# Spectral layer of a four-layer network: six block products for each full Toeplitz product, shifted differences subtracted by GpSimd

## What is computed

```python
U_plus  = causal_conv(phi[:, k], u)                  # u: 2304 tokens, phi: taps of filter k, 16 filters
U_minus = causal_conv(phi[:, k], u * sgn) * sgn      # sgn = +1, -1, +1, ...
out = sum_k s_k * (U_plus @ M_plus[k] + U_minus @ M_minus[k]) + sum_i shift(u, i) @ M_u[i]
# four such sums, on the first T, T/2, T/4 and T/8 tokens, with matrices of their own, are weighted and added
```

## Time and profile before

| what | value |
|---|---|
| three runs, median (lowest to highest) | 8442.53 us (8434.91 to 8447.69) |
| profiled execution: time, span | 8448.98 us, 8447.1 us |
| mean granted TensorE clock | 0.954 of full |
| busy share of the span: TensorE, VectorE, ScalarE, GpSimd | 91%, 63%, 45%, 43% |
| spectral layer, setup to last store | about 6097 to 8447 us |

### The profile page before, as it was taken

One profiled execution on the slowest core, in us unless ns is written; L12 is line 12 of the kernel. 1 busy time (PEld: TensorE's weight loads), 2 busy tenths in 40 slices (PEclk: granted clock), 3 DMA queues, 4 the chain that ended last, 5 costly groups with the idle time before them and its releaser, 6 DMA issues. The chain is left out here.

```text
span 8447.1 us, 141745 instructions
## 1 busy us (share of the span) xinstructions
PE 7665.0 (91%) x51342; PEld 5961.6 (71%) x51342; DVE 5345.4 (63%) x8084; ACT 3817.7 (45%) x8029; POOL 3663.7 (43%) x2420
## 2 busy tenths in 40 slices
PE   8999899997999979999467788699799999999999
PEld 6888678885888858887356677356666666666666
DVE  7999799996999969999445555455532222222222
ACT  5887578873888748876112222244421111111111
POOL 5888468882888828886355554110000000000000
PEclk9999999998999989999689899899999999999999
DMA  2333123331333313332565554000022222222222
GB/s 64 90 91 89 59 75 90 91 88 45 91 90 90 89 44 91 91 90 73 160 181 159 157 156 135 6 3 0 7 89 86 87 91 87 80 94 92 80 86 77
DMA packets 459084, 727.20 MB, mean 86 GB/s; under 512 B 51687, under 2 KB 364040, under 8 KB 456497
## 3 DMA queue, kind: packets, MB, share of 16 engines
q1 hardware_dynamic: 406705, 550.52, 21.1%
q0 software_dynamic: 51840, 169.91, 7.0%
HBM read 686.77 MB, written 33.46 MB: 85 GB/s over the span
## 5 line engine op out<-in xcount | busy, mean ns | idle before, releaser
L591 POOL TENSOR_TENSOR l_arena<-l_arena 128x768 f32<-128x768 f32 x1536 | 2778.7, 1824 | 472.0 <-DVE l_arena L541 411.2
L541 DVE TENSOR_TENSOR_SCAN l_arena<-l_arena,psum 128x384 f32<-128x384 f32 x3072 | 2866.4, 983 | 78.2 <-PE psum L382 42.8
L475 ACT ACTIVATE l_arena<-l_arena,l_A 128x384 f32<-128x384 f32 x3072 | 1665.3, 604 | 81.4 <-DVE l_arena L541 81.3
L384 PE MATMUL psum<-l_arena 128*128 128x128 f32 x11520 | 1581.2, 285 | 28.7 <-DVE l_arena L541 26.2
L384 PEld LDWEIGHTS psum<-l_arena 128*128 128x128 f32 x11520 | 1407.5, 192 | 184.9 <-issue 114.4
L2344 DVE TENSOR_TENSOR st_Uc<-psum,st_both 128x384 f32<-128x384 f32 x512 | 285.5, 558 | 1701.0 <-PE psum L2265 1701.0
L395 PE MATMUL psum<-l_ident,l_arena 128*128 128x128 f32 x9216 | 1260.2, 273 | 53.0 <-ACT l_yT L481 45.5
L395 PEld LDWEIGHTS psum<-l_ident,l_arena 128*128 128x128 f32 x9216 | 1053.7, 141 | 64.3 <-POOL l_arena L591 41.5
L2265 PE MATMUL psum<-st_F,st_xt 128*128 128x384 f16 (+2 forms) x6912 | 1002.1, 290 | 0.0
L2265 PEld LDWEIGHTS psum<-st_F,st_xt 128*128 128x128 f16 x6912 | 649.5, 97 | 385.3 <-issue 62.3
L1148 POOL DMA_INDIRECT l_G<-neighbours,l_idx x648 | 618.6, 955 | 665.4 <-PE psum L1196 325.0
(11 more groups left out here) (397 smaller groups left out, 7668.8 us busy)
## 6 DMA issues: line engine op xcount, KB each, us to landing
l_arena<-c_rows SPq DMA_DIRECT2D x1536, 192.0 KB, 3.0
st_FS<-filter_sums SPq DMA_DIRECT2D x128, 641.0 KB, 7.6
st_F<-filter_parts SPq DMA_DIRECT2D x128, 576.5 KB, 6.4
neighbours<-l_xt SPq DMA_DIRECT2D x256, 72.0 KB
st_mab<-in_st_mp SPq DMA_DIRECT2D x68, 256.0 KB, 7.6
st_mab<-in_st_mm SPq DMA_DIRECT2D x68, 256.0 KB, 7.9
l_G<-neighbours,l_idx POOLq DMA_INDIRECT x648
l_gnx<-in_x SPq DMA_DIRECT2D x4, 1152.0 KB, 5.9
```

The lines of the kernel that those rows point to most:

```text
L384: mm = pe.matmul(ps[:, o:o + P], dtuT[:, g % 2, t, h * P:(h + 1) * P], diagB[:, rank[s] % 3, t, :], start=True, stop=True)
L475: act.activation(decay[:, s % NDC, h, :], dtv[:, g % 2, h, :], ACT.Exp, scale=A[:, g // NRC, h, n:n + 1]).then_inc(s_exp, 1)
L541: dve.tensor_tensor_scan(hbuf[:, n, h, flip], decay[:, s % NDC, h, flip], ps[:, BANK * (2 * (s % 2) + h):BANK * (2 * (s % 2) + h) + RC][:, ...
L591: pool.tensor_tensor(hC[:, s % NHC], hbuf[:, s % NS], Cs[:, s % NCS, :].unsqueeze(1).broadcast_to([P, 2, RC]), ALU.mult).then_inc(s_hc, 1)
```

## The change

Each full product of 3 x 3 blocks is made of six block products. With block taps t(d) and token blocks x0, x1, x2, each row i of the result is t(i-0) x0 + t(i-1) x1 + t(i-2) x2. `own` takes one token block for each row, with the sum of three neighbouring block taps; `pairs` takes three differences of token blocks, each with one block of taps, and each of these three enters two rows, once added and once subtracted. So nine matmuls of 384 columns become 9 + 9 of 128. The results of `own` and of `pairs` lie in banks 5 and 6. The one of the two uses of `pairs` is added in place; the other is shifted by a block, and this *rotated* subtraction is GpSimd's: two `tensor_tensor`, 256 and 128 columns, on `Uc[:, 1]` and again on `Uc[:, 2]`.

The results of mixing now take banks 0 to 4 (the last third in three pieces of 128). The next unit's `shared` and `first` stand ahead of this unit's last mixing. The setup stores five sums of taps (rows of 512) instead of two; `F` shrinks from 1153 to 641 columns, `FS` grows from 2 x 641 to 5 x 385 (for each part, parity and buffer). The token differences (six sets of three blocks) are formed by GpSimd at each batch's start; ordering, transposes and cutting go 384 columns at a time, and ScalarE copies the tokens.

```diff
-FW = HL + 1
+FW = RC + 2 * P + 1
-SW = SR - P + 1
+SW = RC + 1
+SETS, SETW = 5, RC + P
...
             @block.vector
+                st.mark(dve.tensor_tensor(threes[:, 0], tap[:, 0:SETW], tap[:, P:P + SETW], ALU.add))
+                st.link(dve.tensor_tensor(threes[:, 1:3], sums[:, :, 0:SETW], sums[:, :, P:P + SETW], ALU.add))
+                st.mark(dve.tensor_tensor(threes[:, 0], threes[:, 0], tap[:, 2 * P:2 * P + SETW], ALU.add))
+                st.link(dve.tensor_tensor(threes[:, 1:3], threes[:, 1:3], sums[:, :, 2 * P:2 * P + SETW], ALU.add))
+                for at, n, of in ((0, 2, sums[:, :, P:P + SETW]), (2, 3, threes)):
+                    dve.tensor_copy(sets_h[:, at:at + n], of).then_inc(s_th, 1)
...
+                for at, n, of in ((0, 2, sums[:, :, P:P + SETW]), (2, 3, threes)):
+                    dve.tensor_tensor(sets_l[:, at:at + n], of, sets_h[:, at:at + n], ALU.subtract).then_inc(s_th, 1)
...
+                @block.gpsimd
+                def _(pool):
                     for q in range(2):
+                        pool.wait_ge(s_xc, b * 2 * LB + 3 + q)
+                        pool.tensor_tensor(xd[:, q, :], xr[:, q, 0:RC], xr[:, q, RC:2 * RC], ALU.subtract).then_inc(s_xd, 1)
+                    for q in range(2):
+                        src = xr[:, q, 0:2 * RC].rearrange("p (g j s) -> p g j s", g=2, j=LB)
+                        for e, (i, j) in enumerate(((1, 2), (0, 1), (2, 0))):
+                            pool.tensor_tensor(xe[q][:, 0:2, e], src[:, :, i], src[:, :, j], ALU.subtract).then_inc(s_xd, 1)
+                        pool.wait_ge(s_xd, b * 10 + 5 + 4 * q)
+                        pool.tensor_tensor(xe[q][:, 2], xe[q][:, 0], xe[q][:, 1], ALU.subtract).then_inc(s_xd, 1)
...
+                    def own(u, at, three, x0, start):
+
+                        r, z, q, shift = shape(u)
+                        for i in range(LB):
+                            for m, (xpart, fpart) in enumerate(PARTS):
+                                mm = pe.matmul(ps[:, at + i * P:at + (i + 1) * P], xt[:, xpart, x0 + LB - 1 - i, :],
+                                               FS[:, r, fpart, z, three, shift + i * P:shift + (i + 1) * P],
+                                               start=(start and i + m == 0), stop=(i == LB - 1 and m == 2), skip_group_check=True)
+                        return mm
+
+                    def pairs(u, tap, group, start):
+
+                        r, z, q, shift = shape(u)
+                        for e, d in enumerate((0, 2, 1)):
+                            for m, (xpart, fpart) in enumerate(PARTS):
+                                mm = pe.matmul(ps[:, PAIR + e * P:PAIR + (e + 1) * P], xt[:, xpart, PAIR0 + (3 * q + group) * 3 + e, :],
+                                               tap[:, r, fpart, z, shift + d * P:shift + (d + 1) * P],
+                                               start=(start and e + m == 0), stop=(e == 2 and m == 2), skip_group_check=True)
+                        return mm
...
+                        for u in range(2 * NU):
+                            r, q = u // NU, u % 2
+                            done, turned_on = (unit + u) * 4 + 8, (unit + u) * 4 + 4
+                            copied = (unit + u) * 4
+                            pe.wait_ge(s_ea, copied + 2)
+                            own(u, OWN, 3, q * HB + LB, False)
+                            pairs(u, FS[:, :, :, :, 0], 1, False).then_inc(s_cv, 1)
+                            if u % NU == 0:
+                                pe.wait_ge(s_wm[r], use(i, r) + 1)
+                            pe.wait_ge(s_ea, copied + 3)
+                            mix(u, 0)
+                            triangle(u, q * HB + 2 * LB)
+                            own(u, LOW, 4, q * HB, False).then_inc(s_cv, 1)
+                            pe.wait_ge(s_ea, copied + 4)
+                            pairs(u, FS[:, :, :, :, 1], 0, True).then_inc(s_cv, 1)
+                            pe.wait_ge(s_po, turned_on + 2)
+                            mix(u, 1)
+                            v = (u + 1) % (2 * NU)
+                            if not (last and v == 0):
+                                if v % NU == 0:
+                                    pe.wait_ge(s_fl[v // NU], (b * (KF // 2) + i + (1 if v else 2)) * 64)
+                                shared(v)
+                                pe.wait_ge(s_ed, done + 3)
+                                shared_pairs(v)
+                                first(v)
+                            pe.wait_ge(s_po, turned_on + 4)
+                            mm = mix(u, 2)
...
                 @block.vector
+                            dve.wait_ge(s_cv, (unit + u) * 5 + 3)
+                            dve.wait_ge(s_ea, (unit + u) * 4 + 4)
+                            dve.tensor_tensor(second, ps[:, OWN:OWN + RC], pair_1[:], ALU.add).then_inc(s_ed, 1)
+                            if step < 5:
+                                mix_step(i * 2 + r + 1, i + r, 1 - r, step, base + (i * 2 + r + 1) * 8)
+                            dve.wait_ge(s_cv, (unit + u) * 5 + 4)
+                            dve.tensor_tensor(third, ps[:, LOW:LOW + RC], own_s[:, u % 2, :], ALU.subtract).then_inc(s_ed, 1)
+                            dve.wait_ge(s_cv, (unit + u) * 5 + 5)
+                            dve.wait_ge(s_po, (unit + u) * 4 + 4)
+                            dve.tensor_tensor(pair_2[:], ps[:, PAIR:PAIR + RC], pair_s[:, u % 2, :], ALU.subtract).then_inc(s_ed, 1)
+                            dve.wait_ge(s_ed, at + 3)
+                            dve.tensor_tensor(third, third, pair_2[:], ALU.add).then_inc(s_ed, 1)
+                            if step + 1 < 5:
+                                mix_step(i * 2 + r + 1, i + r, 1 - r, step + 1, base + (i * 2 + r + 1) * 8)
...
+                @block.gpsimd
+                def _(pool):
+                    with pool.Fori(0, KF // 2) as i:
+                        unit = (b * KF + i * 2) * NU
+                        for u in range(2 * NU):
+                            for c, step, pair in ((1, 1, pair_1), (2, 4, pair_2)):
+                                pool.wait_ge(s_ed, (unit + u) * 4 + 8 + step)
+                                pool.tensor_tensor(Uc[:, c, P:], Uc[:, c, P:], pair[:, 0:2 * P], ALU.subtract).then_inc(s_po, 1)
+                                pool.tensor_tensor(Uc[:, c, 0:P], Uc[:, c, 0:P], pair[:, 2 * P:], ALU.subtract).then_inc(s_po, 1)
...
                 @block.scalar
+                            act.activation(own_s[:, u % 2, :], ps[:, OWN:OWN + RC], ACT.Copy).then_inc(s_ea, 1)
+                            act.activation(pair_s[:, u % 2, :], ps[:, PAIR:PAIR + RC], ACT.Copy).then_inc(s_ea, 1)
+                            act.wait_ge(s_cv, (unit + u) * 5 + 2)
+                            act.activation(Uc[:, 0, :], ps[:, LOW:LOW + RC], ACT.Copy).then_inc(s_ea, 1)
+                            act.wait_ge(s_cv, (unit + u) * 5 + 3)
+                            act.wait_ge(s_po, (unit + u) * 4 + 2)
+                            act.activation(pair_1[:], ps[:, PAIR:PAIR + RC], ACT.Copy).then_inc(s_ea, 1)
```

More of the change, by code:

```diff
@@ L2155, in pieces, with rows_of, place, totals @@
             return out
+        def rows_of(c):
+            return [(c * RC, (c + 1) * RC)] if c < 2 else [(2 * RC + i * P, 2 * RC + (i + 1) * P) for i in range(3)]
+        def place(p, x):
+            if x < 2 * RC:
+                return BANK * (2 * p + x // RC) + x % RC
+            n = (x - 2 * RC) // P
+            return (BANK * (2 * p + n) + RC if n < 2 else BANK * 4 + P * p) + x % P
+        def totals(p, c):
+            return [(m, lo, hi, place(p, lo)) for r0, r1 in rows_of(c) for m, lo, hi in pieces(r0, r1)]
         with nc.Fori(0, NB) as b:
@@ L2198, in layer3_spectral @@
             with nc.Block() as block:
-                NU, KINDS = 4, ("shared", "first", "second", "third")
-                NG = NU * len(KINDS)
+                NU = 4
+                OWN, PAIR, LOW = (BANK * i for i in (5, 6, 7))
                 USES = (KF // 2 + 1, KF // 2)
@@ new lines, in _, with shape, triangle @@
+                    PARTS = ((0, 0), (0, 1), (1, 0))
+                    def shape(u):
+                        r, z, q = u // NU, u // 2 % 2, u % 2
+                        return r, z, q, (0 if (z and q) else 1)
+                    def triangle(u, x0):
+                        r, z, q, shift = shape(u)
+                        for j in range(LB):
+                            for m, (xpart, fpart) in enumerate(PARTS):
+                                mm = pe.matmul(ps[:, LOW + j * P:LOW + RC], xt[:, xpart, x0 + j, :], F[:, r, fpart, z, shift:shift + RC - j * P],
+                                               start=(j + m == 0), stop=(j == LB - 1 and m == 2), skip_group_check=True)
+                        return mm
@@ new lines, in mix, with shared @@
+                    def mix(u, c):
+                        r, z, q, _ = shape(u)
```

(9 more changed lines are left out.)

233 lines of the change are left out of this document (104 added, 129 removed).

## The result

The changed kernel takes 8224.94 us (median of 4, 8223.19 to 8225.57) where the kernel before, timed beside it, takes 8438.72 (8424.89 to 8447.69): a ratio of 0.9747, 95% interval 0.9731 to 0.9762. 8225 lies in the range of 8125 to 8290, and 49 us above the predicted 8176.

A forecast was written before the change was run, and what follows sets the result against it. TensorE's own work was taken as the bound. Terms of -290 us in the loops, +17 at batch boundaries and +6 in the setup gave -267, from 8449 to 8182 profiled, hence a median of 8176 us, range 8125 to 8290.

The forecast's parts named there:

- TensorE's own work: Spectral layer loops: products, triangles and mixing of one unit on TensorE, 8.42 us before, forecast 7.18 us without waits.
- the 56 ns a short matmul: TensorE's 128-wide f16 matmuls: 56 ns each, taken from runs of three; 62 ns kept for the range.
- a pace set by something else: Rival, chance 0.12: long runs of short matmuls are paced by something else than columns; 62 ns each, 8234 us.
- weight loads not hidden: Rival, chance 0.06: loads in long runs of short matmuls are not hidden; slower from 75 ns each, 8756 at 98 ns.
- the 81 ns that the Trainium skill gives: Load and matmul pairs at 128 columns: 81 ns each would make a unit 1.35 us longer, near 8520 us.
- The waits for GpSimd: TensorE waiting in the loops for GpSimd's subtractions: 0.43 us over four units, 0.11 a unit.
- 0.11 more for each that runs beside VectorE's work on the matrices: GpSimd's pair of subtractions, priced at 1.11 us: 0.11 us dearer when beside VectorE's matrix work.
- mix 1 unwaited: Sign to look for: TensorE's mixing of the middle third starts without waiting for GpSimd's first job.
- the 0.36 at mix 2: Mixing of the last third: 0.36 us late in one unit of four, matrix sums standing ahead on VectorE.
- the first rival: Rival, chance 0.20: GpSimd's jobs take 1.33 us, waits grow by 0.2 us a unit, +51 us, 8227.
- The batch boundary: Outside the loops, per batch: uncovered first and last work, copies, residual additions, ordering block; 4.3 us longer, +17 in all.
- The setup: Before the batches: five sums of taps built and split in place of two, +6 us.

The follow-up runs named there:

- e8: Changed kernel with all matrix steps behind GpSimd's second job and the two 384-wide differences moved to VectorE: 7892.31 us, ratio 0.965 to the kernel before.
- e5: Changed kernel with the two in-loop matrix sums taking one operand from PSUM instead of a loaded matrix (results wrong): 8190.64 us, ratio 0.9665.
- e2: Changed kernel with GpSimd's loop removed and its rotated subtractions done by VectorE, nothing else moved: 8194.12 us, ratio 0.9671.
- e6: The changed kernel unedited, timed again beside e8: 7952.12 us against 8178.44 for the kernel before, ratio 0.9726.

## Why the prediction was right, and where 41 us went

**TensorE's own work** was right. 7.18 us a unit was forecast, 7.20 to 7.26 measured where nobody waits, and the 56 ns a short matmul that the range hung on came out at 57 in runs of eighteen. The rivals of a pace set by something else and of weight loads not hidden fell with it; so did the 81 ns that the Trainium skill gives, as cited in the prediction: the runs of eighteen at 57 ns speak against it.

**The waits for GpSimd** are the term that was mis-sized: 0.11 us a unit forecast, 0.22 measured (7.428 less the 7.204 of e8), 57 us in all for 28. The first units of the filters have 49 of the 57 (7.97 for 7.21, 64 times). The other 8 lie in the second and third units, 7.25 and 7.26 for 7.19 and 7.20, too short to stand in the view of waits; e5 keeps them and e2, with no GpSimd in the loop, does not. The job itself was priced well, 1.15 us for 1.11. The step that failed is "0.11 more for each that runs beside VectorE's work on the matrices": for the pair beside the sums it is 0.38 and 0.44, and VectorE's second sum pays 0.54. With it failed "mix 1 unwaited" and the 0.36 at mix 2, whose part for the order on VectorE e5 shows to be nothing. In e5 queued VectorE operations start before their predecessor's record ends (7124.34, 7124.82), where the sum had gaps of 0.05. So the forecast 28 us stood for a wait at another place than the one that came. The total lies at the number of the first rival, 8227, but not by its mechanism: GpSimd was not slow in all units, it was held up in one of four. The Trainium skill was cited for the shared interface; its page "SBUF — State Buffer" (SBUF: two separate sides) says more, that the pair of ports is "an exclusive lock, not a bandwidth split". The timeline agrees. L2398, which starts first, keeps its 0.68 though GpSimd's first subtraction has started 0.16 behind it, and each of the other three ends its own length less 0.14 behind the one before: 0.59 for 0.73, 0.54 for 0.68, 0.32 for 0.46. No run shows what the 0.14 is.

**The batch boundary** was forecast 4.3 us longer and is 7.1. The miss lies ahead of the first product, which comes 29.9 us behind the first copy in batches 1 to 3, for 24.8 in the mean before: 5.1 longer where 1.7 was forecast (1.5 and 0.2). About 2 of that are the fetched code, 29.9 less 27.9, and this term was missing: the second copy of the pass was read in the diff and costed at nothing. Another 1.1 is a width read wrongly. The last two subtractions of GpSimd's block, L2217, were priced as 128 wide, 0.9 us for both, and are three blocks wide (groups by shape, `st_mab` and `st_Wm` being where the two results lie):

```profile
L2217 POOL TENSOR_TENSOR st_Wm<-st_Wm 128x384 f32<-128x384 f32 x4 | 4.0, 1002 | 0.3
```

So GpSimd's part ends 10.65 us behind the first copy and not at 9.5, and the last split of batch 0 at 12.45 and not at 11.3. Behind the last product the batch is about 2 us longer, for 2.6 forecast.

**The setup** is 5.9 us longer for 6. The loads of filter sums, 962.5 KB in 8.8 us to landing, hold up no pass of the changed kernel. At a batch's start they can, as the forecast allowed; the same kernel in e6 has two such waits (us in total, times, longest), in batches 0 and 3:

```profile
PEld psum L2316 <- DMA st_FS<-filter_sums: 2.8, 2, 2.1
```

So -259 in the loops (32 passes of 59.44 for 67.54), +28 and +6 make the -225 that the profiled spans show, for -290, +17 and +6: of the 41 us 31 are missing in the loops, 11 at the boundaries. The other 8 of the 49 by which the median is off are no work of the kernel: the forecast took 6.5 off the profiled execution to come to the median, and the changed kernel's median stands 2 above it.

## What to carry to other kernels

When work goes to GpSimd, list the VectorE instructions that will run beside it and have both operands in SBUF, and place them where GpSimd's result is not awaited; an operand in PSUM takes them out of the quarrel. When a loop body is written out a second time inside an outer loop, count TensorE's instructions in the outer body: beyond what stays loaded, the jump back costs a late start, here some 2 us a batch. Between the two, a unit by place in its cycle (7.97, 7.25, 7.26, 7.22) says more than a mean.

## What was not expected of the hardware

GpSimd and VectorE slow each other with float32 operations that have one output and two SBUF operands, and VectorE's one-input TENSOR_SCALAR suffers too: L2409 has a median of 284 ns and a longest of 783. The row by line, ns min, median and max:

```profile
L2409 DVE TENSOR_SCALAR st_Wm<-st_Wm,st_mweight x136: 278/284/783, 6184.8 to 8186.6; 128x128 f32<-128x128 f32 x136
...
L2399 DVE TENSOR_TENSOR st_Wm<-st_mab x68: 684/1218/1220, 6184.0 to 8183.7; 128x512 f32<-128x512 f32 x68
```

The kernel before took 8439, 8476, 8178 and 8443 us in the four groups of runs, while the units of the spectral layer agreed to 0.02 us from chip to chip; a difference of 1% is only to be read beside a control on the same chip.
